# Splitting the router of a mixture of experts in halves and reordering the hand-over into it, in an eight-stage kernel

## The chip, the cores and the metric

The kernel runs on one core of one Trainium2 chip. Its time is the device time of one execution in microseconds (us); the median of several runs counts. A core has TensorE (PE: matrix products, PEld: its weight loads), VectorE (DVE), ScalarE (ACT) and GpSimd (POOL) for elementwise work, and SyncE (SP), whose queue starts transfers. Indirect transfers (scatters) are issued by GpSimd.

## The reference

The reference is a chain of eight residual stages on 2048 tokens of 128 features: `x = x + stage(layernorm(x))`. The stages are: a Mamba block, a mixture of 32 experts (top 4), causal attention, a mixture of 8 experts (top 1), windowed attention, a ternary linear layer, a test-time-trained layer, and a mixture of 7 experts. Two of them matter here. The first mixture picks four of 32 experts for a token, within four of eight groups, each expert taking at most 320 tokens in order of arrival:

```
logits = xf @ wg.T;  scores = softmax(logits)
group_scores = max of scores within each of 8 groups
keep the 4 best groups; idx = 4 best experts in them
w = scores[idx] / (sum + 1e-9)
pos = (cumsum(onehot(idx)) * onehot(idx)).sum(-1) - 1;  keep = pos < cap
y[token] += w * (silu(x w1[e]) * (x w3[e])) w2[e];  plus a shared expert
```

The second mixture picks the best of 8 experts, 160 tokens each; tokens beyond that go through a dense overflow network instead. The Mamba block ends with `y * silu(z)` (the gate) and a projection `W_out` that is added to x.

## The kernel before

The 2048 tokens stay in SBUF as 16 tiles of 128 (`k.X`). Every stage is a class with one method per engine (`pe`, `dve`, `act`, `pool`, `sp`); an engine executes its instructions in the order in which these methods issue them, and waits on semaphores (`w.wait_ge`) for the others. So a stage's work can be written into the methods of the stage before it, and the order of the calls is the order of the queue. `w.mark` and `w.own` make VectorE wait for its own last instruction.

**Mamba to first mixture (`Moe32`).** The Mamba stage handles two batches of 1024 tokens by two halves of channels, 16 states each: 64 scans on VectorE (L921). The first batch's result is complete early, and its normalization, features and logits are computed on the side. After the last scan VectorE chooses experts for the first quarter of the tokens (`route_dve(0)`, L1437: softmax, rank of groups to L1477, then the pick from L1479 to L1502), gates the last channel half (`gate_dve(3)`, L863), and computes where the quarter's tokens go (`Dispatch.dve`, L1162 to L1207). Inside that, TensorE counts tokens per expert (`count_pe`, L1150 and L1151) and then projects the second batch (`project_last`, L705). VectorE adds the projection (`out_last_dve`, L878), takes statistics, normalizes eight tiles (`norm_dve`, L1435) and goes on with quarters two to four. TensorE turns these tiles and computes their logits (L1348, L1357). GpSimd copies weights into the rows (L1673) and issues 16 scatters per quarter (`scatter`, L1217), 64 in all, four per tile. Only when all have landed does SP load the experts' rows.

**Attention to second mixture (`Moe8`).** At the end of attention VectorE adds the output of each group of four tiles (`home_dve`, L2080), takes its statistics, and normalizes finished groups for the next stage (`ChunkNorm.chunk_dve`, L385 and L380; the fourth tile of a group goes to GpSimd). TensorE transposes a group (`chunk_pe`, L429), ScalarE copies it (L439), and TensorE computes scores (`scores_pe`, L2781). VectorE chooses for tiles 0 to 7 and 8 to 15 (`shift_dve`, `best_dve`, `which_dve`), but the dispatch is done once, for all 16 tiles, with one count on TensorE. After it GpSimd issues 16 scatters (L1217), of which the ninth and the thirteenth also wait for the first and second output of the overflow network (`behind`). That network runs on TensorE in four chunks: hidden products (L2802), relu on VectorE and ScalarE, outputs (`over_pe`, L2736); VectorE adds an output at L2872.

The same `home_dve` ends windowed attention, in front of the ternary layer (`Ternary`: L429 transposes, L3023 outputs, L3072 the add).

Of the kernel before, what the change touches and what calls it, by code (L numbers as in the profile page):

```python
# [449 lines left out]
class Mamba:  # L450
# [275 lines left out]
    def pe(self, e, w):  # L726
# [52 lines left out]
        self.add_y(e, w, 63)  # L779
        self.after.count_pe(e, w, 0)  # L780
        self.project_last(e, w)
# [100 lines left out]
    def dve(self, e, w):  # L882
# [342 lines left out]
class Moe32:  # L1225
# [7 lines left out]
    def __init__(self, k, before):  # L1233
# [7 lines left out]
        self.early_xnT, self.early_lg, self.nm = early.take(1024), early.take(256), early.take(8)  # L1241
# [6 lines left out]
            g_w=16, stats=4, sd=2, rstd=3, xnv=8, tp=4, fxa=7, **dispatch_signals(4), lg=4, shift=4, probs=4,  # L1248
# [172 lines left out]
    def early_norm_dve(self, e, w):  # L1421
        k, S, h = self.k, self.S, slice(0, 8)
        w.wait_ge(S.sd, 1)
        e.reciprocal(self.rstd[:, h], self.sd[:, h]).then_inc(S.rstd.sem, 1)
        w.wait_ge(S.rstd, 1)
        e.scalar_tensor_tensor(self.nm, k.lnmv[:, h, 0], -1.0, self.rstd[:, h], MUL, MUL).then_inc(S.rstd.sem, 1)

    def norm_dve(self, e, w):
# [8 lines left out]
    def route_dve(self, e, w, h):  # L1437
# [3 lines left out]
        part = lambda t: t[:, t.shape[1] // 4 * h:t.shape[1] // 4 * (h + 1)]  # L1441
        p, gm, rank, keep, km1, mx, sm, s4, r4, idxf, w4, v8, i8 = (part(t) for t in (
            self.p, self.gm, self.rank, self.keep, self.km1, self.mx, self.sm, self.s4, self.r4, self.idxf, self.w4, self.v8, self.i8))
        lg = self.early_lg[:, 128 * h:128 * (h + 1)] if h < 2 else part(k.b(2))
# [32 lines left out]
        w.mark(e.tensor_reduce(rank, gt.rearrange("p (a b) -> p a b", b=8), AX.X, ADD))  # L1477
        w.own()
# [31 lines left out]
    def dve(self, e, w):  # L1510
        k, S = self.k, self.S
        w.all(self.before.ends)
        for h in (2, 3):
            self.route_dve(e, w, h)
# [72 lines left out]

    def early_features_act(self, e, w, c):
        S = self.S
# [45 lines left out]
    def act(self, e, w):  # L1635
# [3 lines left out]
        self.exp_act(e, w, 1)  # L1639
        self.features_act(e, w)  # L1640
# [47 lines left out]
class Attention:  # L1688
# [387 lines left out]
    def home_dve(self, e, w, c):  # L2076
# [2578 lines left out]
```

## Time and profile before

| | |
|---|---|
| median of 3 runs | 1577.28 us (1577.12 to 1578.56) |
| the profiled execution's own time | 1582.03 us |
| its span, first to last instruction | 1580.2 us |
| mean granted TensorE clock | 0.895 of full |
| TensorE busy | 1247.2 us, 79% of the span |
| VectorE busy | 1018.6 us, 64% |
| ScalarE busy | 793.7 us, 50% |
| GpSimd busy | 694.2 us, 44% |

The span is what the trace covers; the execution's own time has a little around it. Busy shares are means over stages with different limits. Of the rows below, a timeline row gives start, duration, engine, line, operation, output and input, and in brackets the idle time of the engine before it with what ended it; `x4` means that four instructions are merged into one row.

### The profile page before, as it was taken

To read this page: it belongs to the slowest core of one execution; us is meant where nothing else is said; L and a number is where in the kernel's file an instruction comes from. 1 tells how busy PE (TensorE), PEld (TensorE's weight loads), DVE (VectorE), ACT (ScalarE), POOL (GpSimd) and SP (SyncE) were. 2 spreads that over 40 slices of the span, in tenths; PEclk is the share of its full clock that TensorE was granted. 3 is DMA by queue.
4 is the path that set the end of the run, shared out by engine and by line. 5 is a ranking of instruction groups with operands and counts; after the bars stand their busy time and mean duration, and the time that the engine had idled before them with its cause. 6 is when DMAs were issued, how large, how long until landed. Compare 5 with 4: busy or idle time off the path is not lost.

```text
span 1580.2 us, 27296 instructions
## 1 busy us (share of the span) xinstructions
PE 1247.2 (79%) x10086; PEld 886.6 (56%) x10086; DVE 1018.6 (64%) x1916; ACT 793.7 (50%) x1634; POOL 694.2 (44%) x688
## 2 busy tenths in 40 slices
PE   6698988224775768878778679988998999984996
PEld 2487777213453324434357434455776777874996
DVE  6998988741112988888553544457976785643774
ACT  5798786102432347767832325546665654321442
POOL 1299986575664430101023310025870881043553
PEclk9699998556887769999979779999999999997999
DMA  6498791112322421211001232111000003001113
GB/s 222 141 290 286 236 363 48 43 49 67 85 79 85 156 98 61 68 56 34 10 25 29 86 127 65 29 40 69 1 0 1 1 1 160 1 31 44 46 46 98
DMA packets 75508, 133.48 MB, mean 84 GB/s; under 512 B 12771, under 2 KB 39846, under 8 KB 74736
## 3 DMA queue, kind: packets, MB, share of 16 engines
q1 hardware_dynamic: 66448, 115.45, 22.0%
q0 software_dynamic: 8064, 13.87, 2.8%
q10 hardware_dynamic: 864, 2.43, 0.4%
q8 instruction: 80, 1.31, 0.3%
q14 instruction: 52, 0.43, 0.1%
HBM read 95.70 MB, written 38.38 MB: 85 GB/s over the span
## 4 chain that ended last, share of the span: by engine, by line
PE 49%; issue 18%; DVE 13%; ACT 9%; DMA 3%; POOL 3%; SPq 3%; another core or an unknown queue 2%; POOLq 0%; DVEq 0%; ACTq 0%
PE ps L1958 6%; PE ps L4197 3%; DVE sb_arena L2024 3%; PE ps L2325 2%; PE ps L718 2%; ACT sb_arena L2272 2%; PE ps L2308 2%; PE ps L2575 2%; PE ps L3278 1%; DVE sb_arena L921 1%; PE ps L4164 1%; PE ps L4165 1%; PE ps L676 1%; PE ps L4166 1%
## 5 line engine op out<-in xcount | busy, mean ns | idle before, releaser
L2024 DVE TENSOR_REDUCE sb_arena<-ps 128x2 f32<-128x1024 f32 (+2 forms) x192 | 211.5, 1131 | 55.5 <-PE ps L2561 32.9
L2272 ACT ACTIVATE sb_arena<-ps 128x512 f32<-128x512 f32 (+1 forms) x320 | 160.3, 554 | 54.7 <-PE ps L2325 51.1
L921 DVE TENSOR_TENSOR_SCAN sb_arena<-ps,sb_arena 128x1024 f32<-128x1024 f32 x64 | 144.3, 2280 | 17.0 <-ACT ps L1018 16.0
L2056 POOL CAST sb_arena<-sb_arena 128x8 bf16<-128x8 f32 (+2 forms) x32 | 6.5, 203 | 287.6 <-DVE sb_arena L2024 149.2
L1958 PE MATMUL ps<-sb_arena 128*32 128x256 f32 (+3 forms) x1856 | 115.4, 356 | 0.2 <-ACT sb_arena L2514 0.2
L1684 POOL DMA_INDIRECT y<-sb_arena x80 | 77.7, 972 | 56.3 <-ACT sb_arena L1633 36.6
L1217 POOL DMA_INDIRECT xe<-sb_arena x80 | 79.0, 987 | 53.4 <-issue 28.8
L1116 POOL TENSOR_TENSOR sb_arena<-sb_Wreg,sb_arena 128x1024 f32<-128x1024 f32 x32 | 75.1, 2377 | 53.2 <-DMA sb_arena<-bcrows 44.8
L718 PE MATMUL ps<-sb_const,sb_arena 128*128 128x128 f32 x768 | 92.3, 276 | 0.0
L718 PEld LDWEIGHTS ps<-sb_const,sb_arena 128*128 128x128 f32 x768 | 89.3, 193 | 0.5 <-issue 0.5
L2325 PE MATMUL ps<-sb_arena 51*128 51x256 bf16 (+2 forms) x768 | 60.4, 248 | 28.3 <-ACT sb_arena L2272 28.2
L2514 ACT ACTIVATE sb_arena<-ps 128x768 f32<-128x768 f32 x64 | 50.2, 785 | 62.2 <-PE ps L2583 62.2
L2308 PE MATMUL ps<-sb_arena 55*128 55x128 bf16 (+4 forms) x576 | 62.0, 292 | 18.9 <-DVE sb_arena L2024 12.3
L3985 POOL TENSOR_TENSOR sb_arena<-sb_arena 128x512 f32<-128x512 f32 x32 | 41.1, 1284 | 79.8 <-ACT sb_arena L3796 59.7
L1116 POOL TENSOR_TENSOR sb_arena<-sb_arena 128x1024 f32<-128x1024 f32 x32 | 74.8, 2365 | 2.6 <-DVE sb_arena L921 2.4
L1029 ACT ACTIVATE sb_arena<-ps,sb_arena 128x128 f32<-128x128 f32 x256 | 69.9, 402 | 11.1 <-PE ps L676 11.1
L676 PE MATMUL ps<-sb_const,sb_arena 128*128 128x128 f32 x384 | 53.9, 284 | 25.2 <-DVE sb_arena L921 10.9
L4351 DVE TENSOR_TENSOR sb_arena<-sb_arena,ps 128x512 f32<-128x512 f32 x60 | 41.0, 688 | 48.6 <-PE ps L4166 25.9
L4482 POOL DMA_INDIRECT y<-sb_arena x44 | 42.9, 975 | 64.6 <-ACT sb_arena L4409 57.9
L676 PEld LDWEIGHTS ps<-sb_const,sb_arena 128*128 128x128 f32 x384 | 44.5, 146 | 38.6 <-issue 28.9
L1958 PEld LDWEIGHTS ps<-sb_arena 128*32 128x32 f32 x1856 | 45.8, 110 | 35.5 <-issue 12.6
L1525 DVE TENSOR_TENSOR sb_arena<-sb_arena,ps 128x320 f32<-128x320 f32 x32 | 15.6, 488 | 76.3 <-ACT sb_arena L1651 32.5
(527 smaller groups left out, 3476.2 us busy)
## 6 DMA issues: line engine op xcount, KB each, us to landing
sb_arena<-bcrows SPq DMA_DIRECT2D x80, 512.0 KB, 6.2
xe<-sb_one SPq DMA_DIRECT2D x31, 260.0 KB, 5.6
sb_Wreg<-e0w SPq DMA_DIRECT2D x24, 256.0 KB, 7.6
sb_arena<-xe SPq DMA_DIRECT2D x16, 325.0 KB
y<-sb_zero SPq DMA_DIRECT2D x20, 256.0 KB, 6.8
sb_Wreg<-e1w SPq DMA_DIRECT2D x16, 256.0 KB, 2.7
sb_Wreg<-e3gu SPq DMA_DIRECT2D x1, 4096.0 KB, 13.8
sb_arena<-y SPq DMA_DIRECT2D x6, 512.0 KB, 4.8
```

Source lines behind the costliest of these rows:

```text
L676: t = e.transpose(k.b(self.C + c)[:, j * 128:(j + 1) * 128], self.hh[i % 3][:, at:at + 128], k.c("ident"))
L718: t = e.matmul(k.b(self.Y + c)[:, at:at + 128], self.hc[i % 4][:, x * 128:(x + 1) * 128], k.c("ident"), start=False, stop=False)
L921: e.tensor_tensor_scan(self.hh[i % 3], k.pair(2 * (i % 2)).rearrange("p c t -> p (c t)"), self.dB[i % 3], 0.0, MUL, ADD).then_inc(S.scan.s ...
L1029: t = e.activation(self.hc[i % 4][:, x * 128:(x + 1) * 128], k.b(self.C + c)[:, j * 128:(j + 1) * 128], ACT.Identity, scale=self.cT[:, b, ...
L1116: e.tensor_tensor(self.dB[i % 3], self.du[b][:, eb, :], self.Bs[i % 6], MUL).then_inc(S.dB.sem, 1)
L1217: e.indirect_dma_start(buf, bass.IndirectOffsetOnAxis(self.iw[:, c:c + 1], 0), xn[q][:, i, :], None, bounds_check=rows - 1, oob_is_err=Fal ...
L1684: e.indirect_dma_start(self.y, bass.IndirectOffsetOnAxis(at, 0), self.ob[u % 3][:, c, :], None, bounds_check=8191, oob_is_err=False).then_ ...
L1958: t = e.matmul(k.b(self.sum_bank(qc))[32 * j:32 * j + 32, o:o + wd], self.vaug[:, b * 8 + kt, 4 * hg + j, :], self.PT[x][:, j, a - q0:a - ...
L2024: e.tensor_reduce(dst, src, AX.X, MAX).then_inc(S.mxr.sem, 1)
L2272: e.activation(self.PT[s % 4][:, 2 * h:2 * h + 2, 0:n], bank[:, :, 0:n], ACT.Exp, scale=self.scale).then_inc(S.ex.sem, 1)
L2308: t = e.matmul(view[:, p, a:z], Q[r, j % 2, tok], KK[r, j % 2, k0 + a:k0 + z], start=True, stop=True, skip_group_check=True)
L2325: t = e.matmul(banks[h][:, j, a:z], KK[r, j, kt * 128:(kt + 1) * 128], Q[r, j, q0 + a:q0 + z], start=True, stop=True, skip_group_check=True)
```

## The change

Four things are changed.

1. In the Mamba stage the choice of a quarter is cut in two, `rank_dve` and `pick_dve`. `gate_dve(3)` stands between the two halves of the first quarter's choice, and on TensorE `project_last` stands in front of the first count.
2. The second batch's eight normalizing instructions move from VectorE to ScalarE (`norm_act`), behind the second quarter's exponential; VectorE computes only the factors.
3. In `home_dve` the normalization of group 1 moves from behind the last home to the front of it. This holds for both attention stages.
4. In the second mixture the choice and the dispatch are done for eight tiles at a time (`choose_dve`, `parts=2`), with a count on TensorE and eight scatters for each. The first half's shift stands before the last group's normalization; the second half's choice stands behind the first chunk of the overflow network's hidden blocks. ScalarE loads the exponential's table before its stage's wait, and TensorE's scores of group 1 stand before the transposes of group 2.

```diff
@@ Mamba.pe
         self.add_y(e, w, 63)
+        self.project_last(e, w)
         self.after.count_pe(e, w, 0)
-        self.project_last(e, w)
@@ Mamba.dve
-        self.after.route_dve(e, w, 0)
+        self.after.rank_dve(e, w, 0)
         self.gate_dve(e, w, 3)
+        self.after.pick_dve(e, w, 0)
         self.after.disp.dve(e, w, 0)
         self.out_last_dve(e, w)
         self.after.norm_dve(e, w)
-        self.after.route_dve(e, w, 1)
+        self.after.rank_dve(e, w, 1)
+        self.after.pick_dve(e, w, 1)
         self.after.disp.dve(e, w, 1)
@@ Moe32.norm_dve
         w.wait_ge(S.rstd, 3)
-        w.wait_ge(self.before.S.dB, 64)
-        for i in range(8, 16):
-            e.tensor_scalar(self.xn[:, i, :], k.X[:, i, :], k.lnmv[:, i, 0:1], self.rstd[:, i:i + 1], SUB, MUL).then_inc(S.xnv.sem, 1)
+        e.scalar_tensor_tensor(self.nm[:, h], k.lnmv[:, h, 0], -1.0, self.rstd[:, h], MUL, MUL).then_inc(S.rstd.sem, 1)
@@ Moe32, new
+    def norm_act(self, e, w):
+        k, S = self.k, self.S
+        w.wait_ge(S.rstd, 4)
+        w.wait_ge(self.before.S.scan, 64)
+        w.wait_ge(self.before.S.dB, 64)
+        for i in range(8, 16):
+            e.activation(self.xn[:, i, :], k.X[:, i, :], ACT.Identity, scale=self.rstd[:, i:i + 1], bias=self.nm[:, i:i + 1]).then_inc(S.xnv.sem, 1)
@@ Moe32.act
         self.exp_act(e, w, 1)
+        self.norm_act(e, w)
         self.features_act(e, w)
@@ Attention.home_dve
         if c == 2:
             self.after.ln.chunk_dve(e, w, 0)
+            self.after.ln.chunk_dve(e, w, 1)
         if c == 3:
-            self.after.ln.chunk_dve(e, w, 1)
             self.after.ln.chunk_dve(e, w, 2)
@@ Moe8.pe
         self.f.chunk_pe(e, w, self.ln.wait_rows, 1)
+        self.scores_pe(e, w, 1).then_inc(S.lg.sem, 1)
         self.f.chunk_pe(e, w, self.ln.wait_rows, 2)
-        self.scores_pe(e, w, 1).then_inc(S.lg.sem, 1)
...
+            if c == 1:
+                self.disp.pe(e, w, 1)
             if c:
                 self.over_pe(e, w, c - 1)
@@ Moe8, in place of route_dve
+    def choose_dve(self, e, w, h):
+        self.best_dve(e, w, h)
+        self.which_dve(e, w, h)
+        w.own()
+        w.mark(e.tensor_copy(self.idxf[:, 8 * h:8 * h + 8], self.i8[:, 8 * h:8 * h + 8, 0]))
+        self.disp.dve(e, w, h)
@@ Moe8.dve
-        self.ln.chunk_dve(e, w, 3)
         w.all(self.before.ends)
-        self.route_dve(e, w)
-        self.disp.dve(e, w)
-        w.wait_ge(S.ir, 1)
+        self.shift_dve(e, w, 0)
+        self.ln.chunk_dve(e, w, 3)
+        self.choose_dve(e, w, 0)
+        self.shift_dve(e, w, 1)
+        self.hidden_over_dve(e, w, 0)
+        self.choose_dve(e, w, 1)
+        w.wait_ge(S.ir, 2)
@@ Moe8.act
         self.ln.act(e, w, ready, (2,))
         self.f.chunk_act(e, w, 0)
+        self.f.chunk_act(e, w, 1)
         self.ln.act(e, w, ready, (3,))
+        load_table(k, e, 5, ACT.Exp)
+        w.all(self.before.ends)
+        self.exp_act(e, w, 0)
+        self.f.chunk_act(e, w, 2)
+        self.f.chunk_act(e, w, 3)
+        self.hidden_over_act(e, w, 0)
+        self.exp_act(e, w, 1)
         for c in range(1, 4):
...
+            self.hidden_over_act(e, w, c)
@@ Moe8.pool
-        self.ln.wait_rows(w, 3)
         e.tensor_copy(self.xq.bitcast(I32)[:, :, 128], k.c("places1")).then_inc(S.ids.sem, 1)
         w.wait_ge(S.ids, 1)
-        self.disp.scatter(e, w, self.xe, [self.xq], self.ROWS, [(k.zeroed, 688)], S.scat, behind={8: [(S.od, 1)], 12: [(S.od, 2)]})
+        for h in range(2):
+            self.ln.wait_rows(w, 2 * h + 1)
+            self.disp.scatter(e, w, self.xe, [self.xq], self.ROWS, [(k.zeroed, 688)], S.scat, h, behind={8: [(S.od, 1)], 12: [(S.od, 2)]})
```

`hidden_over_dve(c)` and `hidden_over_act(c)` are the two relu blocks of chunk c that each engine's loop held before.

## Rows read from the trace of the kernel before

**Rows 1.** The page, costliest groups: count, then busy us, mean ns of one, idle before.

```profile
L1217 POOL DMA_INDIRECT xe<-sb_arena x80 | 79.0, 987 | 53.4 <-issue 28.8
L1029 ACT ACTIVATE sb_arena<-ps,sb_arena 128x128 f32<-128x128 f32 x256 | 69.9, 402 | 11.1 <-PE ps L676 11.1
```

**Rows 2.** Timeline, end of the Mamba stage and the first dispatch.

```profile
264.52 1.88 PE L714 MATMUL ps<-sb_arena,sb_const 128*128 128x512 f32 x4
...
266.96 0.42 DVE L1477 TENSOR_REDUCE sb_arena<-sb_arena 128x32 f32<-128x256 f32 x1
...
270.45 1.21 DVE L863 TENSOR_TENSOR sb_arena<-sb_arena,ps 128x1024 f32<-128x1024 f32 x1
...
272.30 1.02 DVE L1166 TENSOR_REDUCE sb_arena<-sb_arena 128x128 bf16<-128x512 f32 x1
...
273.63 6.29 PE L705 MATMUL ps<-sb_arena 128*128 128x128 f32 x32
...
277.85 0.17 DVE L1206 CAST sb_arena<-sb_arena 128x16 int32<-128x16 f32 x1
...
279.08 1.21 POOL L1217 DMA_INDIRECT xe<-sb_arena  x1 [5.05 <-issue]
279.96 1.28 DVE L878 SCALAR_TENSOR_TENSOR sb_X<-ps,sb_small,sb_X 128x1024 f32<-128x1024 f32 x1 [1.85 <-PE ps L705]
```

**Rows 3.** Windows: length, busy us (instructions) of PE, PEld, DVE, ACT, POOL, granted clock, DMA.

```profile
268.00:270.00 2.00, 0.00 (x0) 0.00 (x0) 1.83 (x17) 1.31 (x2) 0.00 (x0) 0.66 0.00 0
...
279.00:280.00 1.00, 0.92 (x9) 0.73 (x7) 0.04 (x1) 0.00 (x0) 0.92 (x1) 1.00 0.00 0
```

**Rows 4.** Timeline, second batch's normalization and scatters of quarters two and three.

```profile
284.26 2.14 DVE L1435 TENSOR_SCALAR sb_arena<-sb_X,sb_ln,sb_rs 128x128 f32<-128x128 f32 x8
...
301.67 0.29 DVE L1172 COPY sb_arena<-ps 128x128 f32<-128x128 f32 x1 [4.58 <-remote]
...
306.99 0.98 POOL L1217 DMA_INDIRECT xe<-sb_arena  x1 [6.93 <-DVE sb_arena L1206]
...
328.76 0.98 POOL L1217 DMA_INDIRECT xe<-sb_arena  x1 [0.78 <-issue]
```

**Rows 5.** Timeline, causal attention's last home to the second mixture's last scatter.

```profile
800.46 0.69 DVE L2080 TENSOR_TENSOR sb_X<-sb_X,ps 128x512 f32<-128x512 f32 x1 [0.30 <-PE ps L1989]
...
802.56 1.01 DVE L380 TENSOR_SCALAR sb_arena<-sb_X,sb_ln,sb_rs 128x128 f32<-128x128 f32 x3
...
805.61 1.72 PE L2781 MATMUL ps<-sb_small,sb_arena 128*128 128x8 f32 x8
...
807.46 0.22 DVE L2826 TENSOR_TENSOR sb_arena<-ps,sb_small 128x64 f32<-128x64 f32 x1 [1.75 <-PE ps L2781]
...
808.06 3.42 PE L2781 MATMUL ps<-sb_small,sb_arena 128*128 128x8 f32 x16
...
820.36 0.17 DVE L1206 CAST sb_arena<-sb_arena 128x16 int32<-128x16 f32 x1
...
821.39 1.10 POOL L1217 DMA_INDIRECT xe<-sb_arena  x1 [15.22 <-DVE sb_arena L1206]
...
832.82 0.69 DVE L2872 TENSOR_TENSOR sb_arena<-ps,sb_arena 128x512 f32<-128x512 f32 x1 [6.44 <-remote]
...
833.30 3.73 PE L2736 MATMUL ps<-sb_Wreg,sb_arena 128*128 128x128 f32 x32
...
833.51 0.97 POOL L1217 DMA_INDIRECT xe<-sb_arena  x1 [2.09 <-remote]
...
842.44 0.97 POOL L1217 DMA_INDIRECT xe<-sb_arena  x1 [0.30 <-issue]
```

**Rows 6.** Timeline, windowed attention into the ternary layer.

```profile
1051.67 1.11 PE L429 MATMUL ps<-sb_const,sb_Wreg 128*128 128x128 f32 x4 [0.76 <-DVE sb_Wreg L380]
...
1054.62 0.69 DVE L3072 TENSOR_TENSOR sb_X<-sb_X,ps 128x512 f32<-128x512 f32 x1 [0.88 <-PE ps L3023]
...
1057.08 0.69 DVE L3072 TENSOR_TENSOR sb_X<-sb_X,ps 128x512 f32<-128x512 f32 x1 [0.45 <-PE ps L3023]
```

More of the change, by code:

```diff
@@ L1432, in norm_dve, with part, rank_dve @@
         w.wait_ge(S.rstd, 3)
-        w.wait_ge(self.before.S.dB, 64)
-        for i in range(8, 16):
-            e.tensor_scalar(self.xn[:, i, :], k.X[:, i, :], k.lnmv[:, i, 0:1], self.rstd[:, i:i + 1], SUB, MUL).then_inc(S.xnv.sem, 1)
-    def route_dve(self, e, w, h):
+        e.scalar_tensor_tensor(self.nm[:, h], k.lnmv[:, h, 0], -1.0, self.rstd[:, h], MUL, MUL).then_inc(S.rstd.sem, 1)
+    def part(self, h, *tiles):
+        return [t[:, t.shape[1] // 4 * h:t.shape[1] // 4 * (h + 1)] for t in tiles]
+    def rank_dve(self, e, w, h):
         k, S, E = self.k, self.S, self.E
         gt, eq, n = self.gt, self.eq, 4
[L1441 to L1444, printed above, removed]
+        p, gm, rank, mx, sm = self.part(h, self.p, self.gm, self.rank, self.mx, self.sm)
+        lg = self.early_lg[:, 128 * h:128 * (h + 1)] if h < 2 else self.part(h, k.b(2))[0]
         l3 = lg.rearrange("p (i e) -> p i e", e=E)
@@ L1477, in route_dve, with pick_dve @@
         w.mark(e.tensor_reduce(rank, gt.rearrange("p (a b) -> p a b", b=8), AX.X, ADD))
+    def pick_dve(self, e, w, h):
+        E, n = self.E, 4
+        p, rank, keep, km1, s4, r4, idxf, w4, v8, i8 = self.part(
+            h, self.p, self.rank, self.keep, self.km1, self.s4, self.r4, self.idxf, self.w4, self.v8, self.i8)
+        p3 = p.rearrange("p (i e) -> p i e", e=E)
         w.own()
@@ L1513, in dve @@
         for h in (2, 3):
-            self.route_dve(e, w, h)
+            self.rank_dve(e, w, h)
+            self.pick_dve(e, w, h)
             self.disp.dve(e, w, h)
@@ L2888, in dve @@
         k, S = self.k, self.S
+        w.all(self.before.ends)
+        self.shift_dve(e, w, 0)
         self.ln.chunk_dve(e, w, 3)
[L2890 to L2901 removed]
+        self.choose_dve(e, w, 0)
[3 more added lines that the diff above has]
+        w.wait_ge(S.ir, 2)
+        w.mark(e.tensor_scalar(self.nvm, self.disp.keep, -1.0, 1.0, MUL, ADD))
+        for c in range(1, 4):
+            self.hidden_over_dve(e, w, c)
+            self.over_dve(e, w, c - 1)
         for ex in range(8):
@@ L2926, in xT_act, with exp_act, hidden_over_act @@
         e.copy(self.xT[ex % 2], self.k.b(ex % 2)[:, 0:160]).then_inc(S.xT.sem, 1)
+    def exp_act(self, e, w, h):
+        S = self.S
+        w.wait_ge(S.shift, h + 1)
+        e.activation(self.p[:, 64 * h:64 * h + 64], self.p[:, 64 * h:64 * h + 64], ACT.Exp).then_inc(S.probs.sem, 1)
+    def hidden_over_act(self, e, w, c):
+        k, S = self.k, self.S
+        for blk in (1, 3):
+            w.wait_ge(S.oh, 4 * c + blk + 1)
+            w.wait_ge(S.od, c - 1)
+            e.activation(self.ho[c % 2][:, blk, :], k.b(self.over_banks[blk]), ACT.Relu, bias=k.s("ob1")[:, blk:blk + 1]).then_inc(S.oha.sem, 1)
     def act(self, e, w):
@@ L2932, in act @@
         self.f.chunk_act(e, w, 0)
+        self.f.chunk_act(e, w, 1)
         self.ln.act(e, w, ready, (3,))
-        for c in range(1, 4):
-            self.f.chunk_act(e, w, c)
-        w.all(self.before.ends)
-        for h in range(2):
-            w.wait_ge(S.shift, h + 1)
-            e.activation(self.p[:, 64 * h:64 * h + 64], self.p[:, 64 * h:64 * h + 64], ACT.Exp).then_inc(S.probs.sem, 1)
-        for c in range(4):
-            for blk in (1, 3):
-                w.wait_ge(S.oh, 4 * c + blk + 1)
-                w.wait_ge(S.od, c - 1)
-                e.activation(self.ho[c % 2][:, blk, :], k.b(self.over_banks[blk]), ACT.Relu, bias=k.s("ob1")[:, blk:blk + 1]).then_inc(S.oha.sem, 1)
+        load_table(k, e, 5, ACT.Exp)
+        w.all(self.before.ends)
+        self.exp_act(e, w, 0)
[3 more added lines that the diff above has]
+        self.exp_act(e, w, 1)
+        for c in range(1, 4):
+            self.hidden_over_act(e, w, c)
         self.xT_act(e, w, 0)
@@ L4467, in pool @@
         rows = self.iw.bitcast(U32)
-        behind = {8: 5, 12: 7, 16: 9, 20: 11, 24: 13, 28: 14}
+        behind = {8: 5, 12: 7, 16: 9, 20: 11}
         for i in range(NT):
```

31 lines of the change are left out of this document (10 added, 21 removed).

## The prediction, made before the changed kernel was run

> **What bounds the kernel now.** I read the page first, then the chain of waits around the two mixtures of experts, then the timelines of the three places that the diff touches, and last the windows for the clock. The page shows no engine that is the bound of the whole: TensorE is busy 79% of the span, VectorE 64%. So each touched place has to be read for what ends last in it. In both mixtures that is GpSimd: each token copy goes out as an indirect transfer that GpSimd issues, 0.97 us long [rows 1], at a pitch of 1.28 us (one and the 0.30 us before the next). 64 of them fill the stage from 279.08 on in the first mixture, 16 from 821.39 on in the second, and only then can the experts' rows be loaded. What counts there is when the first one starts and how long GpSimd stands between two. The third place, from attention into the ternary layer, has no such chain; VectorE and TensorE hand over to each other in turn.
>
> **Place A, the end of the Mamba stage and the first mixture.** Before, VectorE ranks and picks (rank's last step ends 267.38), gates at 270.45 to 271.66, marks the choice until 273.32, and TensorE counts, and after it projects from 273.63 to 279.92; the first scatter goes at 279.08 [rows 2]. VectorE has then waited 1.85 us for the projection at 279.96.
> The gate moves in front of the pick, so it ends near 268.5 instead of 271.66. Total VectorE work up to the choice is the same 1.21 us plus the same pick, so the choice is still due at 273.3. TensorE can begin the 32 matmuls of the projection at 268.6, 5.0 us earlier, and the count must follow them now. The question is whether they fit in the 4.8 us before 273.4. They took 6.29 us at mostly half clock [rows 2]; at full clock, 9 of them pass in 0.92 us, 0.102 each, 3.3 us for 32 [rows 3]. TensorE has worked until 266.40, so its idle time before the projection shrinks from 7.2 to 2.2 us. In the profile the granted clock fell from 1.00 (2.4 GHz) to 0.50 (1.2 GHz) inside 268 to 270 [rows 3], with the mean of 0.66 placing the fall at 268.6, just where the projection would begin. So the projection costs between 3.3 us (count not late at all) and 6.3 us (count, and the first scatter, late by 1.5 us). I take 5.4 us, between the two and nearer to the slow one because the fall is that near: first scatter 0.6 us late.
> VectorE's second batch then starts when the first dispatch is through: the 1.85 us wait goes, less 0.6, so 1.25 us earlier. ScalarE takes over the eight normalizing instructions: 2.14 us leave VectorE [rows 4] and one small instruction of about 0.2 us comes in, 1.9 us net. On ScalarE eight such instructions cost at most 8 x 0.40 = 3.2 us by its nearest row, the PSUM to SBUF one of 128x128 [rows 1], and at least half of that; they run behind the exponential that the second quarter needs, and what waits for them (eight transposes, two copies, the logits of quarters three and four) sits on TensorE in front of the second count. Those end some 2 us before that count is due, so I price the cover at nothing; without it each us of lateness is a us of the second count.
> The second quarter's indices are thus 3.1 us earlier. What is that worth? GpSimd stood idle for 6.93 us before the second quarter's first scatter at 306.99, and for 0.78 us at the same hand-over before the third quarter's at 328.76, where the indices were long there [rows 4]. So 6.1 us are VectorE's lateness. Of these, 4.58 us is one wait of VectorE for a count that TensorE had finished, released late and by nothing that the trace names [rows 4]. If that wait returns, the gain is 3.1 us, since GpSimd still waits for VectorE; if it does not, GpSimd sets the start itself, 0.6 us later for its late first scatter, and the gain is 5.5 us. And if neither it nor its kind was there in the timed runs, the kernel before had almost no gap to close, and the part costs the 0.6 us. The profiled execution took 1582.03 us and its span 1580.2, so 1.8 us lie around it, while the median is 1577.28: 4.75 us less, about such a wait. So I take A as -1.5 us, between -3.1 and +0.6, with ends at -5.5 and +1.5.
>
> **Place B, attention into the second mixture.** Moving the second group's normalization (three tiles 1.01 us and a reciprocal, 1.2 together) in front of the last home puts that home from 800.46 to about 801.3 [rows 5]; the VectorE work up to the third group is the same, so only the order changes. TensorE's second group of scores, before at 805.61 to 807.33 [rows 5], goes right behind its transposes, at 804.35, and ends 805.4 (full clock) to 806.1 (half clock). The old choice ran from 807.46 to 820.53 [rows 5], 13.1 us: 0.75 for each half's shift, 2.3 of waiting for the exponential, 1.4 and 1.2 for each half's best and which, 0.2 for a cast, and 4.2 for marks, count and indices of all tiles. The new first half needs shift 0.75, last normalization 1.2, best, which and cast 2.8, marks 0.5: chosen at 810.8 to 811.6. The count stands behind the 16 remaining score matmuls on TensorE (3.42 us at half clock [rows 5]), so it passes at 811 to 812.8; 2.9 us of small steps on half the columns bring the indices at 814.1 to 816.0, against 820.53 before. With the same 0.86 us to the first scatter that is 815.0 to 816.9, against 821.39 [rows 5]: 4.5 to 6.4 us earlier. ScalarE's table load and exponential lie under the last normalization.
> Not all of it arrives at the end. The thirteenth scatter waits for the second overflow output, as written. That output ended at 837.03 before [rows 5]. Now TensorE also waits in its middle for the second choice (VectorE: two hidden blocks, 1.5 us, then 2.8 and 0.5): the second count passes at 821.4 to 823.2, first output 3.73, hidden 3.6 and waiting for VectorE to 829.5 or 831.3, second output 3.73 [rows 5], 833.3 to 835.1. Three pitches and 0.97 us later the last scatter is out: 838.2 to 840.0, against 843.41 [rows 5], 3.4 to 5.2 us less. Of the old time, 1.8 us was the wait of the ninth scatter for an output that TensorE had ended (2.09 less 0.30, same kind of wait as in A [rows 5]); without it in the timed runs the gain is 1.6 to 3.4. I take -3.5, ends -5.5 and -1.0. No transfer is added: the 16 scatters leave GpSimd's queue in two groups of eight instead of one, and the load of the rows on the SP queue, then experts and written rows, follow the last of them as before.
>
> **Place C, attention into the ternary layer.** The same swap acts here. TensorE's second transposes waited for VectorE until 1051.67 [rows 6]; their tiles are ready at 1049.8, so TensorE starts at 1050.9, behind a bias matmul. The first output then no longer holds VectorE 0.88 us at 1054.62, nor the second 0.45 us at 1057.08 [rows 6]: 1.33 us, and VectorE carries it to the next stage. Ends: -1.3 and 0, if the home that comes 1.2 us later holds someone.
>
> **Sum.** -1.5 - 3.5 - 1.3 = -6.3 us: 1575.7 for a profiled execution, 1571.0 against the median. The bounds of the parts add to -12.3 and +0.5.
>
> **A rule against it.** More VectorE work now lies under scatters. In the rows a scatter takes 0.97 to 0.98 us with VectorE at work, as the mean of all 80 does, 0.987 [rows 1, 4]; the longest is 1.21 [rows 2]. Eight scatters lengthened by that 0.24 us would cost 1.9 us. The Trainium skill, "SBUF — State Buffer", "Who interferes with whom", says that an indirect transfer's descriptors wait while VectorE holds the port that it shares with GpSimd, with 620 ns becoming some 3100. By that page's factor of five the eight scatters above the second choice of B would cost 8 x 3.9 = 31 us more. By that rule this trace does not go, with its mean of 0.987 us.
>
> **Rivals.**
> (1) *Waits like the 4.58 us one were not in the timed runs*: A gives +0.6, B -2.5, C -1.3: -3.2, 1574.1. For it: the 4.75 us between profile and median. Against: such a wait shows in both mixtures [rows 4, 5]. Chance 0.27.
> (2) *Both gaps close in full*: A -5.5, B -5.2, C -1.3: -12, 1565.3. For it: the projection may run at full clock. Chance 0.10.
> (3) *Slower: TensorE's releases come late where they now count.* Before, VectorE's 6.44 us wait at 832.82 held only what had slack [rows 5]. Now the second mixture's second count is handed to VectorE under running scatters, and TensorE, the thirteenth scatter and the row load hang on it. One stall of 4.6 us there only eats B's 3.5; two, of 4.6 and 6.4, cost 11, -6.3 + 11 = +4.7, 1582. It decides above 6.3 us of new stalls. Chance 0.05.
> (4) *VectorE's work lengthens the scatters under it*: 0.24 us for each of B's eight, +1.9, and for five more of A's, +1.2: -6.3 + 3.1 = -3.2, 1574.1; only first scatters show it. Chance 0.04.
> (5) *The swap at the homes hurts* (homes 1.2 us late at two places, nothing given back): -6.3 + 1.3 + 2.4 = -2.6, 1574.7. Chance 0.04.
> The forecast, partial stalls in both, has 0.50.
>
> **Numbers.** 1571.0 us; its own range 1568.0 to 1574.0. With (1) in and half of (2), the range is 1565.5 to 1575.5. About 0.2% (3.2 us) is what this measurement can tell: faster needs less than 1574.1. Forecast and (2) are nearly all faster, (1) half, (4) and (5) a third: 0.75 faster; 0.19 the same; 0.06 slower.
>
> **What would show it.** Projection before the count on TensorE, starting near 268.6, its length telling the clock; first scatter of A within 1.5 us of the old; VectorE's residual add directly behind the dispatch; the wait before A's seventeenth scatter shorter than 6.93 us. In B a first scatter some 5 us earlier, then a wait of the thirteenth on the second output. In C VectorE's 0.88 and 0.45 us gone. I am wrong if the projection runs past 274.9, if the second count of B comes after 824, or if new unnamed waits stand on GpSimd's path.

## The result, and the profile after

The changed kernel took 1573.69 us (median of 21 runs, 1564.45 to 1582.29) against 1579.62 us for the kernel before on the same chip (21 runs, 1570.08 to 1585.54). The ratio is 0.9964, 95% interval 0.9949 to 0.9978: 5.7 us less, 3.5 to 8.1. The forecast sum was 6.3 us less. The size is the forecast one. **The reason is not.** Most of the gain comes from an edit that the description of the change and the prediction both left out; that the two sizes agree is luck.

That edit is the last hunk of the diff, in the last mixture (7 experts). I call it place D:

```
-        behind = {8: 5, 12: 7, 16: 9, 20: 11, 24: 13, 28: 14}
+        behind = {8: 5, 12: 7, 16: 9, 20: 11}
```

The 25th and the 29th of its 32 scatters no longer wait for VectorE's 13th and 14th product, the last ones of the seven shared blocks that TensorE works on meanwhile.

The page of the changed kernel, costliest groups, with the same columns as [rows 1]; the span went from 1580.2 to 1572.7 us:

```profile
L1219 POOL DMA_INDIRECT xe<-sb_arena x80 | 78.8, 986 | 45.8 <-issue 29.1
L1031 ACT ACTIVATE sb_arena<-ps,sb_arena 128x128 f32<-128x128 f32 x256 | 70.0, 403 | 11.8 <-PE ps L676 11.8
```

A scatter is as long as before, 986 ns against 987 [rows 1], and GpSimd's idle time before scatters fell by 7.6 us.

**Place A** in the timeline of the changed kernel, to be held against [rows 2]. All of it starts 1.52 us later, because the untouched Mamba stage took that much longer in this execution:

```profile
268.48 0.42 DVE L1479 TENSOR_REDUCE sb_arena<-sb_arena 128x32 f32<-128x256 f32 x1
...
268.82 1.21 DVE L863 TENSOR_TENSOR sb_arena<-sb_arena,ps 128x1024 f32<-128x1024 f32 x1
...
270.09 5.47 PE L705 MATMUL ps<-sb_arena 128*128 128x128 f32 x32 [2.17 <-DVE sb_arena L863]
...
275.39 0.22 PE L1152 MATMUL ps<-sb_arena,sb_constb 128*128 128x128 bf16 x1
...
279.84 1.27 DVE L878 SCALAR_TENSOR_TENSOR sb_X<-ps,sb_small,sb_X 128x1024 f32<-128x1024 f32 x1
...
280.91 1.21 POOL L1219 DMA_INDIRECT xe<-sb_arena  x1 [5.36 <-issue]
```

The projection takes 5.47 us with a granted clock of 0.82, 0.50 and 0.66 in the windows that it spans (same columns as [rows 3]):

```profile
270.00:272.00 2.00, 1.91 (x14) 1.92 (x15) 1.86 (x17) 0.83 (x2) 0.00 (x0) 0.82 0.00 0
272.00:274.00 2.00, 2.00 (x11) 2.00 (x11) 1.79 (x8) 0.00 (x0) 0.00 (x0) 0.50 0.00 0
274.00:275.00 1.00, 1.00 (x8) 1.00 (x8) 0.84 (x1) 0.00 (x0) 0.01 (x1) 0.66 0.00 0
```

Further into the first mixture, answering to [rows 4]:

```profile
285.38 3.17 ACT L1604 ACTIVATE sb_arena<-sb_X,sb_arena,sb_rs 128x128 f32<-128x128 f32 x8
...
301.47 0.29 DVE L1174 COPY sb_arena<-ps 128x128 f32<-128x128 f32 x1 [7.46 <-issue]
...
306.79 0.98 POOL L1219 DMA_INDIRECT xe<-sb_arena  x1 [4.58 <-DVE sb_arena L1208]
```

VectorE reached the wait for the second count at 294.02, 29.4 us after the choice began (34.0 before), but stood there 7.46 us instead of 4.58. Most of what it had gained went into a longer wait.

**Place B**, answering to [rows 5]:

```profile
801.53 1.87 PE L2800 MATMUL ps<-sb_small,sb_arena 128*128 128x8 f32 x8 [0.68 <-ACT sb_arena L439]
...
812.57 0.17 DVE L1208 CAST sb_arena<-sb_arena 128x8 int32<-128x8 f32 x1
...
813.62 1.10 POOL L1219 DMA_INDIRECT xe<-sb_arena  x1 [8.13 <-DVE sb_arena L1208]
...
825.99 0.97 POOL L1219 DMA_INDIRECT xe<-sb_arena  x1 [2.33 <-PE ps L2755]
...
832.41 0.97 POOL L1219 DMA_INDIRECT xe<-sb_arena  x1 [1.62 <-PE ps L2755]
...
836.24 0.97 POOL L1219 DMA_INDIRECT xe<-sb_arena  x1 [0.30 <-issue]
```

The first scatter comes 7.8 us earlier by the clock of the trace (5.0 counted from the attention's third home), the last 6.2 (3.4). The ninth and the thirteenth wait for the overflow outputs.

**Place C**, answering to [rows 6]; the 0.88 and 0.45 us are gone:

```profile
1048.94 0.67 DVE L3108 TENSOR_TENSOR sb_X<-sb_X,ps 128x512 f32<-128x512 f32 x1
...
1050.86 0.65 DVE L3108 TENSOR_TENSOR sb_X<-sb_X,ps 128x512 f32<-128x512 f32 x1
```

**Place D.** The kernel before, waits between 1400 and 1470 us: what waited for what, us in all, how often, the longest. These rows stood in its trace when the prediction was made, and the prediction has no term for them:

```profile
ACT sb_arena L4416 <- remote: 16.9, 3, 7.4
...
PE ps L4145 <- DMA sb_arena<-xe: 16.7, 1, 16.7
...
POOL xe L4473 <- DVE sb_arena L4351: 10.6, 2, 6.5
```

and its timeline, from the scatter that waited to the first expert:

```profile
1431.01 1.38 PE L4197 MATMUL ps<-sb_Wreg,sb_arena 128*128 128x128 f32 x10 [0.33 <-issue]
...
1435.53 0.97 POOL L4473 DMA_INDIRECT xe<-sb_arena  x1 [6.53 <-DVE sb_arena L4351]
...
1444.46 0.97 POOL L4473 DMA_INDIRECT xe<-sb_arena  x1 [0.30 <-issue]
...
1446.88 2.94 SPq L4118 DMA_DIRECT2D sb_arena<-xe  x6
...
1449.11 0.66 PE L4145 MATMUL ps<-sb_const,sb_arena 128*128 128x128 f32 x2 [16.72 <-DMA sb_arena<-xe]
```

TensorE stood idle for 16.7 us until the rows were there, and the rows hung on the scatters behind the threshold. After the change, the same waits between 1396 and 1466 us:

```profile
ACT sb_arena L4452 <- remote: 27.4, 3, 17.8
...
POOL xe L4509 <- DVE sb_arena L4387: 4.1, 1, 4.1
```

TensorE's wait for the rows is gone. In exchange ScalarE's unnamed waits (`remote`: the trace knows nothing that released them) grew from 16.9 to 27.4 us, and TensorE itself runs late. Its last 16 output matmuls of the shared blocks took 3.0 us before (1429.41 to 1432.39, ten of them in the x10 row above). Now they take 15.2 us (1425.07 to 1440.26), with gaps of 1.0 to 2.2 us that the trace puts down to no other engine, while the rows are loaded from 1436.84 on:

```profile
1431.37 0.37 PE L4233 MATMUL ps<-sb_Wreg,sb_arena 128*128 128x128 f32 x1 [2.22 <-issue]
...
1436.84 2.95 SPq L4154 DMA_DIRECT2D sb_arena<-xe  x6
...
1438.39 1.87 PE L4233 MATMUL ps<-sb_Wreg,sb_arena 128*128 128x128 f32 x8 [1.04 <-issue]
```

### The profile page after: what moved, and what is told of

Its sections match the earlier page's. It is cut to its first block, busy times and chain, and to the rows that moved or that the text cites. A ratio compares the mean times of both kernels' runs of the same rounds, so it can differ in the third digit from the quotient of the medians.

```text
span 1572.7 us, 27323 instructions
## 1 busy us (share of the span) xinstructions
PE 1250.5 (80%) x10088; PEld 890.1 (57%) x10088; DVE 1018.9 (65%) x1927; ACT 796.4 (51%) x1643; POOL 694.1 (44%) x688
## 4 chain that ended last, share of the span: by engine, by line
PE 51%; issue 16%; DVE 12%; ACT 9%; SPq 4%; DMA 4%; POOL 4%; another core or an unknown queue 1%; DVEq 0%; POOLq 0%; ACTq 0%
PE ps L1977 5%; PE ps L4233 3%; DVE sb_arena L2043 3%; PE ps L2344 2%; POOL sb_arena L1118 2%; ACT sb_arena L2291 2%; PE ps L718 2%; PE ps L2327 2%; PE ps L3314 1%; PE ps L4219 1%; PE ps L4200 1%; PE ps L4201 1%; PE ps L4202 1%; PE ps L3285 1%
## 5 line engine op out<-in xcount | busy, mean ns | idle before, releaser
L2291 ACT ACTIVATE sb_arena<-ps 128x512 f32<-128x512 f32 (+1 forms) x320 | 160.3, 554 | 54.0 <-PE ps L2344 50.1
L921 DVE TENSOR_TENSOR_SCAN sb_arena<-ps,sb_arena 128x1024 f32<-128x1024 f32 x64 | 144.1, 2279 | 16.7 <-ACT ps L1020 15.6
L4021 POOL TENSOR_TENSOR sb_arena<-sb_arena 128x512 f32<-128x512 f32 x32 | 41.1, 1284 | 81.2 <-ACT sb_arena L3832 55.7
L4387 DVE TENSOR_TENSOR sb_arena<-sb_arena,ps 128x512 f32<-128x512 f32 x60 | 41.1, 688 | 48.2 <-PE ps L4202 25.3
L4452 ACT ACTIVATE sb_arena<-ps 128x512 f32<-128x512 f32 x60 | 35.7, 598 | 61.4 <-remote 27.4
```

Source lines behind the costliest of these rows:

```text
L921: e.tensor_tensor_scan(self.hh[i % 3], k.pair(2 * (i % 2)).rearrange("p c t -> p (c t)"), self.dB[i % 3], 0.0, MUL, ADD).then_inc(S.scan.s ...
L2291: e.activation(self.PT[s % 4][:, 2 * h:2 * h + 2, 0:n], bank[:, :, 0:n], ACT.Exp, scale=self.scale).then_inc(S.ex.sem, 1)
```

## Experiments

Each set of runs below was made on one chip, with the kernel before beside it. The chips differ: the kernel before needed 1580.14, 1551.01, 1577.72 and 1548.15 us (medians of sets 2 to 5; set 1 is the result). So ratios are compared, and traces only among sets of the same kind: 1, 2 and 4 (the first kind below), or 3 and 5 (the second). "Kind" names what the traces show in these sets. Each of the chips of sets 2 to 5 served in one of these sets only, so whether it belongs to the chip or to a condition that it was in stays open.

### Set 2: each place alone

Place A alone (hunks 1 to 8 of the diff). Its core:

```
-        self.after.count_pe(e, w, 0)
         self.project_last(e, w)
+        self.after.count_pe(e, w, 0)
```

> Place A alone (first mixture: projection before the first count, last gate between ranking and picking, the second batch's normalizations on ScalarE). My theory: about 1.95 us less from the start of the first choice to the first load of dispatched rows, as between the two traces (0.2 to 3), so 0.12% less time. Rival: the 3 us that the untouched experts behind it gave between the two traces belong to it too (other moments of the 64 scatters, other collisions), then 4 to 5 us. Rival: nothing, the 1.95 us are chance of one execution, as the 1.5 us of the untouched Mamba layer are.

Measured: 1580.41 us, ratio 1.0001 (0.9980 to 1.0021). No gain.

Place B alone (the hunks of the second mixture, without the swap in the attention):

```
-        self.disp = Dispatch(k, A, S, self.idxf, 1, E, CAP, (3, 4))
+        self.disp = Dispatch(k, A, S, self.idxf, 1, E, CAP, (3, 4), parts=2)
```

> Place B alone (second mixture: choice, counts and scatters in two halves). My theory: 3.4 us less (2 to 4.5) from the end of causal attention to the load of the dispatched rows, 0.2% less time, with the first scatter about 5 us earlier and two or three stalls of GpSimd on the overflow outputs that give part of it back. Rival: without the second norm chunk moved earlier in the attention's last home (left out here) the first half's scores come later, and only 1 to 2 us are left.

Measured: 1584.29 us, ratio 1.0019 (1.0000 to 1.0037). Its trace nevertheless shows the gain at the place: 59.56 us from the last load of causal attention to the load of the dispatched rows, against 64.13 in the kernel before.

The swap at the homes alone:

```
             self.after.ln.chunk_dve(e, w, 0)
+            self.after.ln.chunk_dve(e, w, 1)
         if c == 3:
-            self.after.ln.chunk_dve(e, w, 1)
```

> Home swap alone (the second norm chunk of the next stage moved ahead of the attention's last home, in both attentions). My theory: 1.3 to 1.6 us less before the ternary stage, nothing before the second mixture, where the scores still wait for the whole attention: 0.1% less, within what can be measured. Rival: it delays the last home and costs 0.4 us at each place: no change or slightly slower.

Measured: 1580.93 us, ratio 0.9997 (0.9976 to 1.0018).

Place D alone (the hunk shown above):

> The two last thresholds of the last mixture taken away alone: its 25th and 29th scatter no longer wait for hidden blocks 13 and 14. My theory: the load of the dispatched rows comes 4 to 6 us earlier, but TensorE is in its shared blocks until about the same time and the experts start with it, so the end gains 0 to 3 us, likeliest 2. Rival: all of the 6 us reach the end (0.4% less). Rival: nothing reaches it, since VectorE and ScalarE get their releases from TensorE later when scatters run without a pause.

Measured: 1576.43 us, ratio 0.9961 (0.9944 to 0.9977): as much as the whole change, and more than the 0 to 3 us expected. TensorE's idle stretch before the first expert, 15.2 to 17.0 us in the five traces of this kind with all six thresholds, is gone; its longest gap there is 3.4 us. From the first scatter to the seventh load of rows, which waits until TensorE has used a buffer, the five take 74.6 to 75.2 us and the four with D 68.8 to 70.7: 5.0 us less on the mean, and nothing behind it gives that back (97.9 to 99.5 us from there to the load of the results, in all nine). The waits of the kernel with D alone, between 1400 and 1470 us:

```profile
ACT sb_arena L4416 <- remote: 28.7, 5, 17.9
...
POOL xe L4473 <- DVE sb_arena L4351: 3.3, 2, 1.8
```

### Set 3: one place taken out, and two other versions, on another chip

The changed kernel without place B:

```
-        self.disp = Dispatch(k, A, S, self.idxf, 1, E, CAP, (3, 4), parts=2)
+        self.disp = Dispatch(k, A, S, self.idxf, 1, E, CAP, (3, 4))
```

> The changed kernel without place B: the second mixture's choice, counts and scatters in one piece again, everything else changed. If B is worth the 4 us that both traces with it show from the end of causal attention to the load of the dispatched rows, this kernel needs about 1577.5 us, 0.2 to 0.3% more than the changed one (ratio to the kernel before 0.9985 to 0.999). If B alone was slower by 0.19% for a cause of its own, this kernel is the fastest so far, ratio 0.994 to 0.9955. If the 0.19% was chance of twelve executions and B is worth nothing, the ratio is that of the changed kernel, 0.9964.

The changed kernel without place D:

```
-        behind = {8: 5, 12: 7, 16: 9, 20: 11}
+        behind = {8: 5, 12: 7, 16: 9, 20: 11, 24: 13, 28: 14}
```

> The changed kernel with the last mixture's six thresholds as before: places A, B and C together. My theory now: nearly all of the gain comes from the two thresholds taken away, so the ratio to the kernel before is 0.9985 to 1.000, and TensorE idles some 16 us in one piece before the last mixture's first expert, as before. Rival, my forecast on record: A, B and C bring 6.3 us together and the thresholds little, ratio 0.996.

The changed kernel without any threshold in the last mixture:

```
-        behind = {8: 5, 12: 7, 16: 9, 20: 11}
+        behind = {}
```

> The changed kernel without any threshold in the last mixture's scatters. In the changed kernel the 32 scatters take 43.5 us, of which 4.1 us wait at a threshold. My theory: they end some 3 us earlier, but TensorE's first expert no longer waits for their rows, it waits for VectorE's part of the shared blocks, so nothing is gained: same as the changed kernel, ratio 0.9955 to 0.997. Rival: scatters without a pause hold back VectorE and TensorE in the shared blocks, which is what the thresholds were good for, and the first expert starts 1 to 4 us later: ratio 0.997 to 0.999. Rival: the 3 us reach the end, ratio 0.9945.

The changed kernel with a halt of GpSimd in the first mixture:

```
-            self.disp.scatter(e, w, self.xe, self.xq, self.ROWS, [(k.zeroed, 688)], S.scat, h)
+            self.disp.scatter(e, w, self.xe, self.xq, self.ROWS, [(k.zeroed, 688)], S.scat, h, behind={8: [(S.cnt, 2)]})
```

> The changed kernel, with one added wait: in the first mixture's first quarter the ninth scatter waits until TensorE has counted the second quarter. Six traces show VectorE released from that count 2.0 to 7.0 us after TensorE's matmul is over, always while GpSimd issues scatters. Theory, starvation: GpSimd's unbroken scatters keep the release back; with GpSimd halted the count arrives within 0.6 us of the matmul's end, the second quarter's indices are ready before the first quarter's sixteenth scatter, and the gap between sixteenth and seventeenth scatter falls from 2.8 to 7.5 us to under 1 us; the last scatter comes 0 to 3 us earlier, since GpSimd loses about 3 us in the halt. Rival: the delay is TensorE's own (its matmul ends later than the trace models): both engines are released 2 to 7 us late all the same, and the last scatter comes 3 to 6 us later. Time: ratio 0.995 to 0.9965 by the first, 0.998 to 1.000 by the second.

Measured, in this order: 1.0001 (0.9983 to 1.0019), 0.9986 (0.9967 to 1.0004), 0.9992 (0.9973 to 1.0011) and 1.0006 (0.9982 to 1.0029). Nothing can be told from the kernel before, with D or without (1551.00 us with all six thresholds, 1550.84 with none). The version without D lies in the range expected for it, 0.9985 to 1.000, but that says nothing of D here, since the versions with D lie there or above as well. The expectations did not allow for a chip on which the long waits do not exist. VectorE's and ScalarE's waits that the trace puts down to nothing it knows ("remote") sum to 122.5 us in the kernel before on its first chip, and to 102 to 172 us in the eight other traces of sets 1, 2 and 4. In the five traces of sets 3 and 5 they are 0.0 us. The second count of the first mixture reaches VectorE at once. The version without place B, in its timeline:

```profile
291.31 0.31 PE L1153 MATMUL ps<-sb_arena,sb_constb 128*128 128x128 bf16 x1
291.66 0.29 DVE L1174 COPY sb_arena<-ps 128x128 f32<-128x128 f32 x1 [0.49 <-PE ps L1153]
```

And the last mixture's 32 scatters take 40.3 and 40.4 us from the first issue to the last with all six thresholds (40.1 with none), against 49.6 to 50.1 on the other chips: VectorE's hidden blocks are done before the scatters that ask for them. TensorE waits for the rows all the same, with the thresholds (first row, the version without place D) and without them (second row, the one with no threshold):

```profile
PE ps L4181 <- DMA sb_arena<-xe: 12.9, 1, 12.9
```

```profile
PE ps L4181 <- DMA sb_arena<-xe: 12.8, 1, 12.8
```

The halt had nothing to repair here. It cost what it holds: the first mixture takes 106.5 us from the choice to the load of rows, 103.4 to 104.1 in the other four traces of this kind. So whether a halt brings late releases forward was not tested where they are late. The timeline of that version shows the halted ninth scatter:

```profile
292.36 0.29 DVE L1174 COPY sb_arena<-ps 128x128 f32<-128x128 f32 x1 [0.49 <-PE ps L1153]
...
293.11 0.97 POOL L1219 DMA_INDIRECT xe<-sb_arena  x1 [3.69 <-PE ps L1153]
```

### Set 4: both kernels again, and the second mixture without its thresholds

The kernel before and the changed kernel, unchanged; the third is the changed kernel with this edit:

```
-            self.disp.scatter(e, w, self.xe, [self.xq], self.ROWS, [(k.zeroed, 688)], S.scat, h, behind={8: [(S.od, 1)], 12: [(S.od, 2)]})
+            self.disp.scatter(e, w, self.xe, [self.xq], self.ROWS, [(k.zeroed, 688)], S.scat, h)
```

> The kernel before, unchanged, for a trace of it beside the changed kernel's on the same chip. Two sets of runs differ by 29 us for this same kernel (medians 1580.1 and 1551.0). Theory: in the slower set the semaphore releases are 2 to 18 us late wherever GpSimd issues indirect transfers, and the three mixtures hold nearly all of the 29 us. If this run is of the quicker set: first mixture from the choice to the load of rows about 105.5 us (1.5 more than with place A), its experts 116 to 119 us, the last mixture's 32 scatters 40.1 us with all six thresholds in place. If it is of the slower set: 104 to 109, 131 to 135 and 49.5 to 50.1 us. Rival: the 29 us lie in all stages alike.

> The changed kernel, unchanged. If the set is the quicker one: the thresholds of place D cost nothing there, so only A, B and C are left, some 1.5, 3 and 1 us by the traces, ratio 0.9965 to 0.9985, nearer the second since three kernels with them gave 0.9986, 0.9992 and 1.0006. If it is the slower one: 0.9964 again, within 0.0015. Rival: the change brings 0.36% whatever the set.

> The changed kernel without the two thresholds in the second mixture's scatters (9th behind the first overflow output, 13th behind the second). Theory: the scatters run at 1.28 us each, 3 to 4 us of stalls are gone and the load of dispatched rows comes that much earlier; of this 0 to 2 us reach the end, because TensorE has its four overflow chunks to finish first: ratio 0 to 0.001 under the changed kernel's. Rival: all 3 to 4 us reach the end, 0.002 to 0.0025 under it. Rival: scatters without a pause hold the overflow work back and the first expert starts later: the same or slower than the changed kernel.

This chip is of the first kind: the profiled execution of the kernel before took 1577.46 us, with 131.15 us for the first mixture's experts and 49.68 for the last mixture's scatters. The changed kernel: 1570.90 us, ratio 0.9954 (0.9938 to 0.9971), so the result repeats, 7.3 us less. The kernel before again, at the place of the 4.58 us wait of [rows 4]:

```profile
296.33 0.29 DVE L1172 COPY sb_arena<-ps 128x128 f32<-128x128 f32 x1 [0.49 <-PE ps L1151]
```

The same instruction of the same kernel waited 4.58 us in one execution and 0.49 in another. In the changed kernel on this chip (its profiled execution, 1578.59 us, is the slowest of its eight) a wait of the same sort fell elsewhere, where no other engine has a part. VectorE finds the indices (last at 340.04), copies them, and between the two waits only for its own counter:

```profile
340.04 0.20 DVE L1501 FIND_INDEX8 sb_arena<-sb_arena 128x8 uint32<-128x32 f32 x1
...
346.37 0.17 DVE L1504 CAST sb_arena<-sb_arena 128x16 f32<-128x16 uint32 x1 [6.13 <-remote]
```

Without the thresholds in the second mixture: 1573.78 us, ratio 0.9981 (0.9955 to 1.0007). That is between the kernels and no better than the changed one; the two intervals overlap, so no loss against it is shown either. The load of the dispatched rows came 2.9 us earlier (56.24 us after attention's last load, 59.14 in the changed kernel), but from there to the load of the results it took 44.70 us instead of 37.19. Its trace says where: with the scatters running through, TensorE's second group of 32 output matmuls takes 12.6 us, from 825.8 on, and 3.7 us in each of the thirteen other traces:

```profile
828.71 0.40 PE L2755 MATMUL ps<-sb_Wreg,sb_arena 128*128 128x128 f32 x2 [1.71 <-issue]
...
833.67 0.37 PE L2755 MATMUL ps<-sb_Wreg,sb_arena 128*128 128x128 f32 x1 [1.03 <-issue]
```

In the same stretch, to 834.6, ScalarE stands 16.8 us and VectorE 11.7 us in waits in the overflow work that the trace puts down to nothing (7.1 and 4.8 us are the longest of these two lines in the changed kernel's two traces):

```profile
ACT sb_arena L2962 <- remote: 16.8, 1, 16.8
...
DVE sb_arena L2897 <- issue: 11.7, 1, 11.7
```

### Set 5: places A, B and C together once more

> Places A, B and C together once more, thresholds of the last mixture as before. On two sets of the slower kind the whole change gave 0.9964 and 0.9954, and place D alone 0.9961, so A, B and C should give 0.998 to 1.000 here, wherever this set falls; on the quicker set they gave 0.9986. Rival, my forecast's sum of 6.3 us: 0.996. If the trace is of the slower kind: TensorE idles 12 to 17 us in one piece before the last mixture's first expert, and the wait for the second quarter's count in the first mixture is again anywhere from 2 to 7 us. From the end of causal attention to the load of rows 58.3 to 59.6 us, as in the five traces with place B (61.2 to 64.2 in the six without).

Measured, on a chip of the second kind: 1550.73 us against 1548.15, ratio 1.0013 (0.9997 to 1.0030). With set 3's 0.9986 the mean of the two is 1.000: no gain from A, B and C that could be told there. The changed kernel itself was not run on a chip of the second kind, and A, B and C together without D not on one of the first. No version was shown to beat the changed kernel.

## Why the prediction was right in its number and wrong in its cause

**The time.** 1573.69 lies in the range and the ratio matches the sum, but the sum was made of the wrong terms, so the agreement is luck. A, B (without the swap) and the swap, each alone on a chip of the first kind, measured +0.01%, +0.19% and -0.03%; all together without D, on two chips of the second kind, -0.14% and +0.13%. The forecast for them was -0.40%. The -6 us are D, with 0.9961 alone against 0.9964 and 0.9954 for the whole change; it stood in the diff and had no term at all. The step that failed first is the reading of the change.

**Place A, -1.5 us.** The parts were sized well. The projection would start 5.5 us after the choice's start (it did, 270.09 - 264.58) and take 5.4 us (5.47; in the two traces in which the clock stayed at 1.00 throughout, 3.84 us, where the forecast's lower bound was 3.3). The first scatter would be 0.6 us late (16.33 us after the choice's start against 16.02, 0.3 late). VectorE's 1.85 us wait went. ScalarE's eight norms cost 3.17 us (at most 3.2 forecast). VectorE reached the wait for the second count 2.8 us sooner, 29.4 us after the choice's start on the mean of four traces of the first kind with A, 32.2 of the five without (3.1 forecast). The step that failed is "if that wait returns, the gain is 3.1 us". It takes a late release for a fixed length added behind TensorE's work. The VectorE waits of these traces were 7.5, 3.6, 5.9 and 7.5 us with A, and 4.6, 0.5, 5.9, 2.5 and 4.0 without: 2.6 us longer on the mean. The seventeenth scatter came 41.0 us after the choice's start with A, 41.3 without. In two of the four traces with A (the changed kernel, and the one without thresholds in the second mixture) the release, at 301.47 and 299.36, falls on the end of the sixteenth scatter, as if it stayed where it is while the wait before it grows. It is not shown as a mechanism. The warning sign "the projection runs past 274.9" came true (275.56), by the 1.52 us of the later start.

**Place B, -3.5 us.** At the place it was right: from attention's last load to the load of rows 59.1 to 59.6 us in three traces of the first kind with its thresholds, 61.8 to 64.2 in five without B, -3.6 us on the means; 58.3, 58.3, 58.4 and 59.1 against 61.2 on the other kind of chip, -2.7. The first scatter came 5.3 us sooner on the means of the first kind (4.5 to 6.4 forecast), the thirteenth waited for the second overflow output as forecast, and the second count at 819.91 was well before 824. But the time did not follow: 1.0019 with B alone, and on the quicker chips the version without B (1.0001) cannot be told from those with it (0.9986 to 1.0013). The step that failed is the unwritten one that what this place gives reaches the end.

**Where B's time goes** is not settled. It is not given back in the second mixture, whose experts take 37.1 to 38.5 us with B and its thresholds and 38.0 to 40.2 without B. A candidate is TensorE's clock at the start of the test-time training layer. Windows of the kernel before, behind its start at 1067.00, then of the changed kernel, behind 1060.74 (the granted clock stands behind the five busy times):

```profile
1077.00:1087.00 10.00, 5.60 (x17) 3.77 (x18) 5.43 (x9) 6.22 (x12) 1.13 (x3) 0.70 0.00 0
1087.00:1097.00 10.00, 9.35 (x48) 6.75 (x47) 9.52 (x17) 5.27 (x12) 6.96 (x6) 0.96 0.00 0
```

```profile
1070.74:1080.74 10.00, 5.60 (x16) 3.78 (x17) 5.04 (x9) 5.83 (x11) 1.07 (x2) 0.63 0.00 0
1080.74:1090.74 10.00, 9.34 (x42) 6.92 (x41) 8.73 (x15) 5.55 (x12) 5.81 (x5) 0.85 0.00 0
```

From that start to the last mixture's first scatter the four traces of the first kind with neither B nor C take 327.3 to 329.3 us, the five with one of them 328.9 to 330.8: 1.7 us more on the means, in code that the change does not touch. That covers half of B at best. Nor is the low clock B's or C's alone: the trace with D alone, which has neither, has 0.69 and 0.80 in the same two windows and is the longest of its four. And single traces vary by more: causal attention, untouched as well, took 273.5 to 277.0 us in eleven traces and 279.9 to 280.9 in three.

**Place C, -1.3 us.** Both waits went. From windowed attention's last load to VectorE's first instruction in the layer behind the ternary one it is 1.1 us on the means of the first kind: 40.3 us in four traces with the swap (39.6 to 41.0), 41.3 in five without (41.1 to 41.6). The ratio of the swap alone is 0.9997, and 1.1 us are too few to show in it.

**Rivals.** (1) said that unnamed waits were missing from the timed runs. On the chips of sets 1, 2 and 4 they were not missing: all nine traces have them. On the two others they were, and there A, B and C gave nothing that could be told, less than the 3.2 us of that rival. (2), some 12 us less, lies outside the 3.5 to 8.1 measured. (3), late releases that land where they now count, is what happened to A, without making the kernel slower. (4) is refuted, 986 against 987 ns for a scatter. The rule of the Trainium skill ("SBUF — State Buffer", "Who interferes with whom") did not show here: B's first eight scatters, with VectorE at work on indices, hidden blocks and the second choice, took 1.10, 0.98 and six times 0.97 us. That section ties the lock to some of VectorE's operations and modes; which of these ran beside the scatters was not separated. (5) is not seen.

**What D's term would have been.** TensorE's 16.7 us wait for the rows says that the last scatter sets the start of the experts, and GpSimd's 6.53 us at the 25th scatter say what can go (the other 4.1 of its 10.6 us stand at an earlier threshold, and still do). Measured are 6.3 to 7.4 us at the last scatter (49.8 on the mean to 43.5 and 42.4) and 5.0 at the experts. What is missing between the two is TensorE's own lateness. With the scatters running on, its last 16 output matmuls of the shared blocks took 12.0 to 15.3 us in the four traces with D, 2.0 to 4.1 in the five without, and 1.95 in all five of the second kind. So the first transposes of rows came 5.7 us earlier on the means and not 6.6 as the last scatter did, and they no longer waited for the rows. The longest unnamed wait of ScalarE in the shared blocks rose with it, from 7.4 us in the kernel before to 17.9 with D alone. The last threshold let TensorE finish first and then wait for the rows; without it TensorE is slower and the rows are earlier. The sum of the two is the gain.

## What to carry to other kernels

Read every hunk of a diff to its last line, and for each one ask the trace which engine stands idle behind it: TensorE's 16.7 us wait in the last mixture lay behind the hunk that had no term. A wait that is released late is not a term that can be kept while the work ahead of it is shortened; where it shows, price the edit at nothing until an experiment says otherwise. And a threshold that only paces transfers is worth what the chip makes of it: two of them cost 0.39% on one kind of chip, and on another even all six cost nothing that could be told. In the second mixture the first kind's TensorE fell behind as soon as its two were gone (in the one trace of it, 12.6 us for matmuls that else take 3.7), and the 2.9 us by which the rows were loaded earlier did not reach the end.

## What was not expected of the hardware

Chips that run the same kernel differ by 29 us, 1.8%, and the difference lies in a few places. Between two traces with the same code up to the last home of causal attention (place A alone, and the changed kernel without B), the first mixture's scatters and experts took 240.3 and 222.1 us, the second mixture 103.6 and 99.3, and the last mixture's 32 scatters 50.0 and 40.1; the stretches between stayed within 2.3 us. These are the stages in which GpSimd issues indirect transfers one after the other while other engines work. The page's last chain has a share of 2% for "another core or an unknown queue" and 18% for "issue" on the first kind of chip (the kernel before):

```profile
PE 49%; issue 18%; DVE 13%; ACT 9%; DMA 3%; POOL 3%; SPq 3%; another core or an unknown queue 2%; POOLq 0%; DVEq 0%; ACTq 0%
```

and none and 9% on the second (the changed kernel without D, set 3):

```profile
PE 54%; DVE 11%; ACT 9%; issue 9%; POOL 7%; DMA 6%; SPq 3%; POOLq 0%; DVEq 0%; ACTq 0%
```

On the first kind the unnamed waits of VectorE and ScalarE are up to 20.3 us long, and VectorE even waited 6.13 us for its own counter. TensorE stands as well, between matmuls of one group that wait for nothing named: its 16 output matmuls of 15.2 us in the last mixture and its 32 of 12.6 us in the second. So it is not one engine alone that is late. Neither stretch has a packet of the two instruction queues of the profile (none from 1410 to 1440 us in the changed kernel, none from 818 to 838 in the version without thresholds in the second mixture), so no code was being loaded in them. What holds the engines and the releases back on those chips stays open.
